# Attention of 16 heads of width 8: head pairs in two row halves of TensorE, the position bias by matmul from one table, paired maxima in one reduction, bias written to PSUM by ScalarE, loops written out

## The reference

```python
x = x + layernorm(attention(layernorm(x)))
x = x + layernorm(ffn(layernorm(x)))

# attention: 16 heads of width 8, 256 x 256 scores per head and sequence
qkv = x @ W_qkv + b_qkv
scores = einsum('bihd,bjhd->bhij', q, k) / sqrt(8) + rel_bias[clip(i - j + 128, 0, 256)]
out = einsum('bhij,bjhd->bihd', softmax(scores), v) @ W_out + b_out

# ffn: 128 -> 512 -> 512 -> 512 -> 128, weights -1, 0 or 1 with a scale for each output
h = silu(x @ w1.T * s1) * (x @ w2.T * s2)
h = gelu(h @ h1.T * s);  h = gelu(h @ h2.T * s);  y = h @ w3.T * s
```

## Time and profile before

| | |
|---|---|
| Runs (us) | 376.62, 391.94, 393.99; median 391.94 |
| Profiled execution | span 400.7 us, 6207 instructions; no other time of this execution is given |
| TensorE (PE) busy | 342.0 us, 85% of the span |
| VectorE (DVE) busy | 250.9 us, 63% |
| ScalarE (ACT) busy | 179.8 us, 45% |
| GpSimd (POOL) busy | 64.4 us, 16% |
| Granted TensorE clock | mean 0.852 of full speed |
| Chain that ended last | PE 66%, issue 15%, DVE 8%, ACT 6%, DMA 3% |

### The profile page before, as it was taken

One profiled execution on the slowest core, in us unless ns is written; L12 is line 12 of the kernel. 1 busy time (PEld: TensorE's weight loads), 2 busy tenths in 40 slices (PEclk: granted clock), 3 DMA queues, 4 the chain that ended last, 5 costly groups with the idle time before them and its releaser, 6 DMA issues.

```text
span 400.7 us, 6207 instructions
## 1 busy us (share of the span) xinstructions
PE 342.0 (85%) x1842; PEld 230.6 (58%) x1842; DVE 250.9 (63%) x1022; ACT 179.8 (45%) x268; POOL 64.4 (16%) x59
## 2 busy tenths in 40 slices
PE   0818869999999999999999998799487799899970
PEld 0514546655666666666666665465266577678850
DVE  4795954334577788777887778384047574373645
ACT  1445122222235344353443534543156866777760
POOL 2780340000010000100001000710023120030111
PEclk9978655555699999999999999555859999999996
DMA  7789993303033303333033305200000000000001
GB/s 203 273 192 286 171 339 132 53 2 54 0 56 55 52 13 43 53 53 52 15 39 53 53 0 182 108 2 0 3 1 2 0 1 0 2 0 26 26 2 53
DMA packets 24068, 26.55 MB, mean 66 GB/s; under 512 B 2928, under 2 KB 20848, under 8 KB 23792
## 3 DMA queue, kind: packets, MB, share of 16 engines
q1 hardware_dynamic: 22272, 24.53, 26.9%
q10 hardware_dynamic: 1776, 1.77, 1.3%
HBM read 19.87 MB, written 6.29 MB: 65 GB/s over the span
## 4 chain that ended last, share of the span: by engine, by line
PE 66%; issue 15%; DVE 8%; ACT 6%; DMA 3%; POOL 1%; SPq 1%; POOLq 0%; ACTq 0%; DVEq 0%
PE st L977 16%; PE st L982 12%; PE ms L952 10%; PE pv L996 10%; PE misc L960 3%; PE misc L1007 3%; PE ms L1099 2%; DVE y_and_z L485 2%; PE ms L1100 2%; DVE ring L680 1%; DMA bias_added<-ext 1%; DMA xs<-x 1%; PE misc L1020 1%; ACT ring L783 1%; PE st L1099 1%
## 5 line engine op out<-in xcount | busy, mean ns | idle before, releaser
L532 DVE CUSTOM_DVE_ANT_0 ms<-ms,big 128x256 f32<-128x256 f32 x240 | 94.7, 454 | 48.1 <-issue 25.0
L783 ACT ACTIVATE ring<-st 128x1024 f32<-128x1024 f32 x64 | 65.5, 1024 | 122.4 <-PE st L982 91.8
L977 PE MATMUL st<-room,identr 128*128 128x512 f32 x192 | 68.4, 486 | 0.0
L952 PE MATMUL ms<-room 32*128 32x256 f32 x240 | 51.1, 336 | 6.1 <-DVE mx L532 5.3
L982 PE MATMUL st<-room 33*128 33x256 f32 x256 | 54.5, 343 | 0.0
L982 PEld LDWEIGHTS st<-room 33*128 33x128 f32 x256 | 40.1, 220 | 23.7 <-issue 21.9
L952 PEld LDWEIGHTS ms<-room 32*128 32x128 f32 x240 | 37.2, 212 | 25.6 <-issue 17.2
L390 POOL TENSOR_TENSOR rstd<-mv,mhalf 128x2 f32<-128x2 f32 (+1 forms) x24 | 20.0, 834 | 168.8 <-DVE mv L482 168.8
L977 PEld LDWEIGHTS st<-room,identr 128*128 128x128 f32 x192 | 38.8, 225 | 13.4 <-issue 3.3
L996 PE MATMUL pv<-ring,v_near 128*9 128x256 f32 x512 | 40.4, 441 | 1.9 <-ACT ring L783 1.9
L1099 PE MATMUL ms<-room,w_hi 128*128 128x512 f32 (+1 forms) x96 | 38.4, 400 | 1.2 <-ACT ring L861 0.7
(11 more groups left out here) (106 smaller groups left out, 438.2 us busy)
## 6 DMA issues: line engine op xcount, KB each, us to landing
room<-q_parts SPq DMA_DIRECT2D x32, 128.0 KB, 4.3
room<-k_parts SPq DMA_DIRECT2D x32, 128.0 KB, 4.5
big<-ext_max SPq DMA_DIRECT2D x2, 1536.0 KB, 9.6
big<-h SPq DMA_DIRECT2D x2, 1024.0 KB, 6.6
ring<-ext ACTq DMA_DIRECT2D x2, 768.0 KB, 6.7
k_parts<-z_parts SPq DMA_DIRECT2D x6, 256.0 KB, 4.1
k_parts<-w_hi SPq DMA_DIRECT2D x6, 256.0 KB, 4.8
xs<-x SPq DMA_DIRECT2D x4, 256.0 KB, 5.8
```

Source lines behind the costliest of these rows:

```text
L532: last = nc.vector.tensor_tensor_reduce(out=tile[:, k, :], in0=tile[:, k, :], in1=reverse(bias_max[:, h, WIN - S - col:WIN - col]), scale=1.0,
L783: nc.scalar.activation(probs[:, s % PRING, :, :, :].rearrange("p k j n -> p (k j n)"), st[s % 2][:, :, :].rearrange("p k n -> p (k n)"), A ...
L952: last = mm(tile[:, k, :], rows(q_rows, par, h, 0)[:, it * P:(it + 1) * P], rows(k_rows, par, h, 0), start=True, stop=True)
L977: mm(st[s % 2][:, k, :], identr[:, :], windows(table[:, a, 2 * s + k, :], 0, P, 2, S), start=(a == 0), stop=False)
```

## The change

- Slot s now holds heads s and s+8 (`SLOT_HEAD`), one in each set of rows, and its matmuls alternate between row 0 and row 64 and write to different PSUM banks.
- `ms` is one tile of two banks for a whole slot, instead of two tiles. The bias for the maxima is added by TensorE (`max_bias`, two matmuls of 512 columns with the identity, high part only), and VectorE takes the negative maxima of the pair with one reduction over 128x1024 values. `bias_max` and its loads are gone. To read one table for both, the queries are stored in reverse order.
- The bias of the scores comes by four identity matmuls in slots 0, 1 and 4 (`BY_PE`), and behind the scores, not ahead of them; in slots 2, 3, 5, 6 and 7 ScalarE copies the bias from `raw` into `st` ahead of the scores, after the exponential two slots before. VectorE adds no bias any more.
- Order on TensorE in a slot: `max_scores`, `scores`, `max_bias`, `score_bias`, then the other work.
- `load_rows` and `load_mrow` have twice as many DMAs of half the size; the copies `v_near` on GpSimd are gone; the ones rows are set in two parts, one ahead of the front and one after it.
- The feed-forward weights have a place of their own (`w_lo`) and are loaded in batch 0. `g_parts` is a ring of three chunks.
- All loops are written out, and the VectorE instructions that held its queue in loops (`hold`) are gone.

```diff
-            def maxima(b, s, first=False):
-                for it in range(TPB):
-                    tile = ms_first[2 * (s % 2) + it] if first else ms[it]
-                    hold(ms_ready, b * (2 * PAIRS) + (2 * s + it + 1))
-                    for k in range(2):
-                        h = 2 * s + k
-                        col = P - it * P
-                        last = nc.vector.tensor_tensor_reduce(
-                            out=tile[:, k, :], in0=tile[:, k, :], in1=reverse(bias_max[:, h, WIN - S - col:WIN - col]), scale=1.0,
-                            scalar=-3.4e38, op0=ALU.add, op1=ALU.max, accum_out=mx[:, it, h:h + 1])
-                    last.then_inc(ms_read, 1)
+            def maxima(b, s):
+                dve.wait_ge(ms_ready, b * PAIRS + s + 1)
+                nc.vector.tensor_reduce(
+                    mx[:, s // RPAIRS, :, :, s % RPAIRS].rearrange("p i k -> p k i"),
+                    max_tile(b, s)[:, :, :].rearrange("p k (i n) -> p k i n", i=TPB),
+                    AX.X, ALU.max, negate=True).then_inc(ms_read, 1)
...
+            def write_bias(b, s):
+                act.wait_ge(exp_done, b * PAIRS + (s - 1))
+                nc.scalar.copy(st[s % 2][:, :, :].rearrange("p k (j n) -> p k j n", j=2),
+                               pair_windows(raw[:, :, :], s)).then_inc(bias_set, 1)
...
                     probabilities(b, s)
+                    ahead = b * PAIRS + s + 2
+                    if ahead < B * PAIRS and ahead % PAIRS not in BY_PE:
+                        write_bias(ahead // PAIRS, ahead % PAIRS)
...
+            def max_scores(b, s):
+                if s % RPAIRS == 0:
+                    pe.wait_ge(rows_in[s // RPAIRS][b % 2], (b // 2 + 1) * ROW_DMAS * 16)
+                if b == 0:
+                    if s >= 2:
+                        pe.wait_ge(ms_read, s - 1)
+                else:
+                    pe.wait_ge(ms_read, b * PAIRS + s)
                 for it in range(TPB):
+                    for half in range(2):
+                        mm(max_tile(b, s)[:, half, it * S:(it + 1) * S],
+                           rows(q_rows, b, half, s, 0)[:, it * P:(it + 1) * P], rows(k_rows, b, half, s, 0),
+                           start=(it == 0), stop=False, skip_group_check=True)
+            def max_bias(b, s):
+                for half in range(2):
+                    last = mm(max_tile(b, s)[:, half, :], identr[:, :],
+                              windows(table_hi[:, 2 * s + half, :], 0, P, 2, S),
+                              start=False, stop=True, skip_group_check=True)
+                last.then_inc(ms_ready, 1)
...
+            def scores(b, s):
+                if s % RPAIRS == 0:
+                    pe.wait_ge(mrow_in[s // RPAIRS], (b + 1) * MROW_DMAS * 16)
+                if s in BY_PE:
+                    if not (b == 0 and s < 2):
+                        pe.wait_ge(exp_done, b * PAIRS + (s - 1))
+                else:
+                    pe.wait_ge(bias_set, biases_by_act(b, s))
+                for j in range(2):
+                    for half in range(2):
+                        last = mm(st[s % 2][:, half, j * S:(j + 1) * S],
+                                  rows(k_rows, b, half, s, 1)[:, j * P:(j + 1) * P], rows(q_rows, b, half, s, 1),
+                                  start=(s in BY_PE and j == 0), stop=False, skip_group_check=True)
+                if s not in BY_PE:
+                    last.then_inc(st_ready, 1)
...
+                    if more:
+                        max_scores(b + 1, s)
+                    scores(b, s)
+                    if more:
+                        max_bias(b + 1, s)
+                    if s in BY_PE:
+                        score_bias(b, s)
+                    if s == 0 and b > 0:
+                        weighted(b - 1, GROUPS - 1)
+                    if s >= 2 and s % 2 == 0:
+                        weighted(b, s // 2 - 1)
...
             store_parts(0)
+            for r in range(RANGES):
+                load_rows(0, r)
+            for c in range(1, NCH):
                 store_parts(c)
+                if c == 1:
+                    for r in range(RANGES):
+                        load_rows(1, r)
+            load_mrow(0, 0)
...
+            for i, (at, src) in enumerate(((W1, w1), (W2, w2), (W_H1, h1), (W_H2, h2), (W3, w3))):
+                sp.dma_start(w_lo[:, at:at + src.shape[-1]], src).then_inc(ffn_w_in[i], 16)
```

More of the change, by code:

```diff
@@ L34 @@
 TPC = CH // P
+BPC = CH // S
 NK = HID // P
@@ L280, in build, with biases_by_act @@
         GPLACE = (0, 1, 1, 0)
+        def biases_by_act(b, s):
+            return b * (PAIRS - len(BY_PE)) + sum(i not in BY_PE for i in range(s + 1))
         @block.sync
@@ L453, in _ @@
             gate_low(3)
-            with pool.Fori(0, NCH) as c:
+            for c in range(NCH):
                 inv_std(c + NCH + 2 * B + 1, TPC)
@@ L613, in _ @@
             for s in range(PAIRS):
-                dve.wait_ge(max_bias_in[s // (PAIRS // 2)], 16)
-                maxima(0, s, first=True)
-            dve.wait_ge(added_in, 16 * len(ADDED))
-            def batch(b, par, post=True, more=True):
+                maxima(0, s)
+            dve.wait_ge(out_w_in, 32)
+            for b in range(B):
                 for s in range(PAIRS):
-                    if not more:
+                    if b + 1 < B:
+                        maxima(b + 1, s)
+                    else:
@@ L628, in batch @@
                         if s == 6:
-                            residual(b - 1)
-                    if more:
-                        maxima(b + 1, s)
-                    if s in ADDED:
-                        add_bias(b, s)
-                    if post and s == 6:
-                        second_norm(b - 1)
-                    if post and s == 7:
-                        z_low(b - 1)
-            batch(0, 0, post=False)
-            with dve.Fori(0, (B - 2) // 2) as i:
-                batch(i * 2 + 1, 1)
-                batch(i * 2 + 2, 0)
@@ L643, in _ @@
-            batch(B - 1, 1, more=False)
+                            second_norm(b - 1)
+                        if s == 7:
+                            z_low(b - 1)
             dve.wait_ge(w_low_max_set, WPIECES)
@@ L801, in weights_high @@
                 nc.scalar.copy(w_hi[:, cols], w_lo[:, cols]).then_inc(w_hi_set, 1)
-            act.wait_ge(table_lo_set, GROUPS - 1)
-            def batch(b, par, first=False, more=True):
+            act.wait_ge(qk_lo_set, 2 * NCH)
+            for b in range(B):
                 for s in range(PAIRS):
@@ L890, in _ @@
             gates_split(NCH)
-            with act.Fori(2, NCH) as c:
+            for c in range(2, NCH):
                 layer(c, 0)
@@ L984, in scores, with score_bias, weighted @@
+            def score_bias(b, s):
+                if b == 0:
+                    pe.wait_ge(table_lo_set, BY_PE.index(s) + 1)
+                for half in range(2):
+                    for part in (table_hi[:, 2 * s + half, :], table_lo[:, LOW_AT_SLOT[2 * s + half], :]):
+                        last = mm(st[s % 2][:, half, :], identr[:, :], windows(part, 0, P, 2, S),
+                                  start=False, stop=True, skip_group_check=True)
                 last.then_inc(st_ready, 1)
-            def weighted(b, par, g, first=False):
+            def weighted(b, g):
@@ L1039, in _ @@
             pe.wait_ge(psum_zeroed, 1)
-            pe.wait_ge(ms_read, 2 * PAIRS)
-            def batch(b, par, first=False, more=True):
+            pe.wait_ge(ms_read, PAIRS)
+            for b in range(B):
+                more = b + 1 < B
+                if b == 1:
+                    pe.wait_ge(ones_set, 4)
                 for s in range(PAIRS):
                     if more:
-                        max_scores(b + 1, 1 - par, s)
+                        max_scores(b + 1, s)
[4 more added lines that the diff above has]
+                        score_bias(b, s)
+                    if s == 0 and b > 0:
+                        weighted(b - 1, GROUPS - 1)
+                    if s >= 2 and s % 2 == 0:
+                        weighted(b, s // 2 - 1)
@@ L1070, in batch @@
-                    if s == 2 and not first:
-                        back(b - 1, 1 - par, 1)
-                    if s == 3 and not first:
-                        heads_T(b - 1)
+                        if b > 0:
+                            pe.wait_ge(mrow_set, b * RANGES + 2)
+                            back(b - 1, 0)
+                    if b > 0:
+                        if s == 2:
+                            back(b - 1, 1)
+                        if s == 3:
+                            heads_T(b - 1)
+                        if s == 4:
+                            project(b - 1)
@@ L1182, in ffn @@
                 tokens_back(0)
-                with pe.Fori(2, NCH) as c:
+                for c in range(2, NCH):
                     layer1(c, exact)
```

467 lines of the change are left out of this document (177 added, 290 removed).

## The result

The changed kernel took 406.0 us (median of four executions, 403.8 to 406.9) where the kernel before took 391.6 (median of four, 376.6 to 394.0). The medians differ by 3.7%. The kernel before has a quicker and a slower state (376.6 us against 391 to 394), and with the slower executions left out the recorded ratio is 1.082, 95% interval 1.071 to 1.092: slower by either count. The forecast was 382. The profiled execution took 406.1 us with a span of 404.2, so the rest, 1.9 us, lies around the span.

The account below looks back on a forecast made before the run. Attention was taken as bound by TensorE. Front 0, batch 0 -6, batch 1 -3, five batches +9, last batch -10 and feed-forward 0 sum to -10, from the median of 391.94 to 382 us; 8-in-10 range 362 to 412.

Parts of the forecast that it names:

- The group of score matmuls: TensorE in attention: four score matmuls in two row halves take 0.43 us at full clock instead of 0.66.
- the halves don't overlap: Rival, chance 0.17: score matmuls in different row halves don't run together, a group stays at 0.63 us; 406 us in all.
- The new wait, at full clock: TensorE waits for VectorE's reduction of the single tile `ms` before the next `max_scores`; with slot 1's wait, 4.4 us a batch.
- VectorE and ScalarE: A VectorE reduction over 1024 takes 1.22 us; a ScalarE bias write takes 1.02 us and is hidden.
- Front, batch 1, last batch, feed-forward block: Stage terms: front 0, batch 1 -3 us, last batch -10 us (bound by ScalarE), feed-forward block 0.
- Batch 0: First attention batch: 36 us all at low clock, about 24 all high, taken as 34, so -6 us.
- the rival with the early clock: Rival, chance 0.20: clock comes up early, last batch at full clock, batch 0 in 24 to 27 us; 365 us in all.
- Five batches, +9: Batches 2 to 6: 22.3 us of TensorE work plus 4.4 of waits, 26.7 us each, 1.8 more than before.
- The clock falls in the new waits: Rival, chance 0.15: waits in slots 5 to 7 lower TensorE's clock, seven us more a batch, +44; 426 us in all.
- the row at 346 to 350: Earlier trace, cited against a falling clock: TensorE busy 2.25 of 4.00 us with full-array matmuls, and the clock stayed.
- the row at 248 to 251: Earlier trace, cited for a falling clock: TensorE busy 1.58 of 3.00 us, still at 1.00; the clock fell in the last batch.
- I carry the difference over unchanged: Baseline step: the profiled span of 400.7 us lies 8.8 above the median of 391.94, and this difference was kept.

Follow-up runs that it names:

- experiment 9: Changed kernel with scores issued first in a slot and TensorE's score biases in slots 1, 4 and 7: 368.1 us, beside 431.9 for the changed kernel.
- Experiment 1: Changed kernel with eight unread 256-column filler matmuls behind the bias of the maxima in slots 3, 5, 6 and 7: 383.5 us.
- experiment 12: Kernel before, with the maxima's scores made to wait until VectorE has read the tile directly before: 559.5 us, beside 375.3 for the kernel before.
- experiment 13: Kernel before, run again unchanged for its profile: 395.1 us.

## Why the prediction was wrong, step by step

- **The group of score matmuls:** 0.43 us, as taken; pairs start within 0.01 us. The rival "the halves don't overlap" is out. The Trainium skill ("TensorEngine Tiling (Array Packing)", "Key Properties") says that different tiles can load weights and multiply in parallel. The trace agrees for two row halves, 0.43 us against the 0.66 of the earlier trace rows.
- **The new wait, at full clock:** right. Forecast 4.4 us a batch in slots 1, 3, 5, 6 and 7; measured (20.1 + 2.3) / 5 = 4.5, with 0.5 in slot 6 instead of 0.9 and 1.1 to 1.2 in 3, 5 and 7. TensorE's work, forecast 22.3, is 21.9 in a batch at full clock (experiment 9). Experiment 1, at clock 1.00, has a batch of 26.7 us, as forecast.
- **VectorE and ScalarE:** 1.226 and 1.017 us against 1.22 and 1.02. ScalarE's writes are hidden.
- **Front, batch 1, last batch, feed-forward block:** 0, -3.0, -10.3, -0.2 against 0, -3, -10, 0. For the last batch the agreement is luck. The prediction had it bound by ScalarE, with 23 us of work; the chain that ended last runs there mostly over TensorE at the low clock (mean 0.66) and then over VectorE, with ScalarE in it for about 3.4 of 28 us. Four pieces of that chain in a row (start, length):

```profile
272.43 0.72 PE st L891 x4
273.15 2.00 PE st L902 x4
275.15 1.83 PE pv L913 x16
276.98 1.17 PE misc L937 x4
```

- **Batch 0:** -12.5 against -6. The clock came up at 60.7 us, earlier than I took it to; 27.3 us is just over the 24 to 27 of the rival with the early clock.
- **Five batches, +9: this failed.** It was +29.5, and the error in it is the clock. The prediction said "PEclk is 1.00 in batches 2 to 6", and gave its opposite, "The clock falls in the new waits", 0.15. That rival had the mechanism, the sign and half of the place: it named slots 5 to 7, but the clock also fell behind slot 3. Of its 34 us a batch and 426 in all, the first trace had 30.8 and 406, the later one 34.1 and 433. What misled me was the row at 346 to 350 of the earlier trace rows, a single gap with the clock kept; I set it against the row at 248 to 251, behind which the clock had fallen. That a gap which returns in every batch is tried against the clock in every batch is my reading of it; what sets these gaps apart from that one (1.75 us, among 512-column matmuls) was not tested. The other "against", that the slots hold full-array 512-column matmuls, didn't help: experiment 12 has four of them in most slots and runs at 0.54.
- **"I carry the difference over unchanged": this failed too.** The profiled execution of before (400.7) was 8.8 us over its median. By experiment 13, where a span 7.7 us shorter has a higher clock in batch 0 and in the last batch, it was long by its clock in these two; no execution at the median has a trace. The changed kernel has no such gap (404.2 + 1.9 against 406.0). Profile against profile the change costs 3.5 us, medians against medians 14. Of the 24.0 us between forecast and median, 20.5 are the five batches, 10.5 are this step (the 8.8 taken off and the 1.8 by which the median is over the span), batch 0 gives 6.5 back and the small terms 0.5.

The Trainium skill, "TensorE: Matmul & The Clock Gate", section "HAM oscillation — how this bites in real kernels", describes a kernel in which a wait for a DMA of some 3 to 5 us returns in every turn of its loop, and the clock falls each time. The trace agrees that recurring waits bring falls in every batch, but here they are waits of 1.2 us at most for VectorE, and not each of them brings one. So the page names the mechanism of the rival, and its sizes would not have led to it.

## What to carry to other kernels

Where TensorE is the bound and its clock is at 1.00, price a new wait twice: by its length, and by what the next dense stretch costs at half the clock. Look at a batch slot by slot for the thinnest stretch, not at the busy share of the stage, and put work that must be done anyway into it: moving one of three bias groups (from slot 0 to slot 7) and issuing the scores first took the changed kernel from 431.9 to 368.1 us with the same number of instructions on each engine. And before a sum starts from one profiled execution, see at what clock it ran against those that were timed.

## What I had not expected of the hardware

With a gap of 0.97 us in every slot, the kernel before has a granted clock of 0.54 in batches 2 to 6 instead of 1.00 and takes 560 us instead of 375. Without a gap its clock can stay at 0.50 too, for 49.8 us in batches 0 and 1. One program settles into patterns of falls that repeat batch by batch (30.8 us in one trace, 34.1 in another), so four executions within 1% (403.8 to 406.9) were no sign of a steady kernel: the next four took 411 to 433. And four matmuls in two row halves take 0.43 us in whichever order they are issued.
